# Next block's K projection and first Q projection issued before the channel-mix K product

## The reference

```python
h = _layernorm(x)
q = _rope(h @ Wq.T + bq); k = _rope(h @ Wk.T + bk); v = h @ Wv.T + bv   # 16 heads of 64
a = banded_attention(q, k, v, window=512) @ Wo.T + bo                   # each query sees 512 keys back
x = x + _layernorm(a)
h2 = _layernorm(x)
h2_prev = h2 shifted by one token
xr = mu_r * h2 + (1 - mu_r) * h2_prev
xk = mu_k * h2 + (1 - mu_k) * h2_prev
y = sigmoid(xr @ Wr) * (square(relu(xk @ Wk2)) @ Wv2)
return x + _layernorm(y)
```

## Time and profile before

| | |
|---|---|
| time | 5608.96 us, median of 2 runs (5575.37 and 5642.55) |
| profiled execution | 5639.6 us |
| its span, slowest core (core 4) | 5637.9 us; the cores span 5570.8 to 5637.9 us |
| busy: PE, DVE, ACT, POOL | 59%, 45%, 38%, 19% |
| one block in the middle (core 4) | 347.8 us |
| of it: Q, K and V projection | 59.3 us |
| attention | 122.6 us |
| Wo | 22.0 us |
| from the last Wo to the first Wr matmul | 68.7 us |
| Wr, Wk2, Wv2 | 32.5, 18.7, 24.0 us |

### The profile page before, as it was taken

The page is one execution under the profiler, slowest core; times in us unless marked ns, Lnnn a source line. Parts: engine busy times, 40 slices in busy tenths (PEclk is TensorE's granted clock), DMA queues, the critical chain, the costliest instruction groups (busy, mean ns, idle before and its releaser), DMA issues.

```text
span 5637.9 us, 53990 instructions; the slowest of 8 cores (5570.8 to 5637.9 us)
## 1 busy us (share of the span) xinstructions
PE 3308.2 (59%) x11681; PEld 1268.3 (22%) x11840; DVE 2528.0 (45%) x3689; ACT 2121.4 (38%) x3905; POOL 1066.1 (19%) x900
## 2 busy tenths in 40 slices
PE   0345737467363756738475583865838377383773
PEld 0112313122121322313121231322313122131321
DVE  2354535444363544535445353443535535354352
ACT  0142534426333342533425253352533326243262
POOL 0011212212111121212212121121211212122131
PEclk9957567585676757566575656756567575666756
DMA  6513031130312213031130312203022130311301
GB/s 198 153 37 103 11 88 62 45 105 1 94 56 83 67 45 105 1 90 60 45 105 26 89 36 67 83 30 99 22 71 79 47 103 8 90 53 50 100 8 60
DMA packets 251425, 376.92 MB, mean 67 GB/s; under 512 B 149730, under 2 KB 149730, under 8 KB 251108
## 3 DMA queue, kind: packets, MB, share of 16 engines
q1 hardware_dynamic: 185060, 163.72, 11.3%
q0 software_dynamic: 33792, 134.22, 7.5%
q10 hardware_dynamic: 32256, 75.51, 3.5%
HBM read 264.33 MB, written 75.50 MB: 60 GB/s over the span
## 4 chain that ended last, share of the span: by engine, by line
PE 35%; DVE 20%; ACT 19%; issue 9%; DMA 7%; POOL 5%; SPq 3%; ACTq 2%; DVEq 1%; POOLq 0%
PE pb L477 8%; ACT pk L449 7%; PE pb L442 5%; PE pb L391 5%; DVE ybuf L489 4%; PE pb L653 4%; PE pb L628 4%; ACT vext L249 4%; ACT vext L252 4%; PE pb L533 3%; DVE ax L589 3%; SPq L173 3%; POOL pk L460 2%; POOL ybuf L702 2%; DVE qx L585 2%
## 5 line engine op out<-in xcount | busy, mean ns | idle before, releaser
L489 DVE RECIPROCAL ybuf<-pb 1x512 bf16<-1x512 f32 x256 | 858.0, 3351 | 772.1 <-PE pb L477 763.4
L628 PE MATMUL pb<-WS,qx 128*128 128x512 bf16 x1008 | 305.4, 468 | 1316.9 <-DVE qx L596 1098.0
L449 ACT ACTIVATE pk<-pb,neg 128x512 bf16<-128x512 f32 (+3 forms) x1792 | 945.4, 528 | 282.5 <-PE pb L442 27.9
L442 PE MATMUL pb<-qx,krot 64*128 64x512 bf16 (+3 forms) x1792 | 675.8, 433 | 308.9 <-ACT pk L449 253.7
L477 PE MATMUL pb<-pk,vext 128*65 128x128 bf16 (+3 forms) x2368 | 522.1, 404 | 78.9 <-DVE ax L502 38.8
L628 PEld LDWEIGHTS pb<-WS,qx 128*128 128x128 bf16 x1024 | 112.9, 114 | 1505.4 <-issue 1463.9
L464 POOL TENSOR_TENSOR pk<-pk,tri4s 128x512 bf16<-128x512 bf16 x256 | 294.8, 1151 | 755.3 <-ACT pk L449 755.3
L460 POOL TENSOR_TENSOR pk<-pk,tri0s 128x512 bf16<-128x512 bf16 x192 | 221.1, 1152 | 1126.7 <-ACT pk L449 1126.7
L340 PE MATMUL pb<-hfm,Wwq 128*128 128x512 bf16 x1008 | 271.3, 428 | 266.2 <-DMA hfm<-hstage 223.4
L477 PEld LDWEIGHTS pb<-pk,vext 128*65 128x65 bf16 x2368 | 309.2, 171 | 254.8 <-issue 171.4
L678 PE MATMUL pb<-WS,pk 128*128 128x512 bf16 x992 | 291.5, 460 | 127.7 <-DVE pk L689 64.3
(11 more groups left out here) (97 smaller groups left out, 3896.4 us busy)
## 6 DMA issues: line engine op xcount, KB each, us to landing
xsl<-x SPq DMA_DIRECT2D x128, 512.0 KB, 3.8
WS<-wo_bf POOLq DMA_DIRECT2D x16, 2048.0 KB, 11.4
WS<-wr_bf POOLq DMA_DIRECT2D x16, 2048.0 KB, 18.9
...
```

The lines of the kernel that those rows point to most:

```text
L442: qlo=qlo, qhi=qhi: e.matmul(pb[bk][:, qlo:qhi], ksrc[po:po + 64, BS * md + 128 * tc:BS * md + 128 * (tc + 1)], qx[po:po + 64, BS * md + q ...
L449: texp = cop("scalar", lambda e, bk=bk, c=c, qlo=qlo, qhi=qhi, pku=pku: e.activation(out=pku[:, BS * c + qlo:BS * c + qhi], in_=pb[bk][:, ...
L489: t_rc = cop("vector", lambda e, rb=recipb[uslot], ub=ub: e.reciprocal(rb, pb[ub][64:65, :]), waits=[t_av, buf.get(("recip", uslot)), prev ...
L628: ins = e.matmul(pb[bk][:, :], qx[:, BS * ci + 128 * tj:BS * ci + 128 * (tj + 1)], WS[1][:, D * ci + BS * hh:D * ci + BS * (hh + 1)], star ...
```

## The change

1. `planA(it + 1)` reads the transposed layer norm into `vext[par2]` (the V buffer of the next block) and no longer into `hfm`.
2. A new `planB1(it + 1)` stands between Wr and Wk2: all four K pairs of the next block (banks (4, 5) and (6, 7) in turn) with their four ropes on DVE, and the matmuls of the first Q pair (banks 0 and 1) without their rope.
3. A new `planB2` opens the next block: the rope of the first Q pair, then the Q pairs 1 to 3 in the banks (6, 7), (4, 5), (6, 7), each with its rope, then V. Since its input lies where V is to be written, V now keeps all eight groups in the eight banks; a memset on DVE (the ones column) waits for all of them, and the eight copies on ACT follow it.
4. The tables of cosine and sine are loaded twice in a block, for K and for Q, with one rope and not two between a load and the rope after next.
5. The square after the relu of Wk2 goes from DVE to POOL. Wk2 uses the banks 2 and 3 (before 4 and 5), Wv2 the banks 2 and 3 (before 6 and 7).
6. The unread output of the layer norms goes to `krot[1 - par]`, in the final layer norm to `ax`; waits follow. The waits of the transposing read of `h2` are now the earlier store and the last use of `hfm`. A debug output (`dbg`) is off.

The rotation (`_rope`) and the projection matmuls (`_proj_mms`) have the same instructions as before, apart from the buffer they read.

```diff
+        buf["lnstat"] = t2
...
-    def planA(it2):
+    t_av_last = None
+    t_attn_evac = []
+
+    def planA(it2, av_tok):
         rows0a = (it2 // NB) * S + (it2 % NB) * BS
+        par2 = (it2 % NB) % 2
...
-        t_hr = [dmat("sync", "hfm", hfm[:, BS * c:BS * (c + 1)], hstage[:, 128 * c:128 * (c + 1)],
-                     waits=[t_hw[-1], buf.get("hfm")]) for c in range(8)]
-        return t_ln, t_hw, [t_hr[-1]] * 8
+        hv = vext[par2]
+        t_hr = [dmat("sync", "hfm", hv[:, BS * c:BS * (c + 1)], hstage[:, 128 * c:128 * (c + 1)],
+                     waits=[t_hw[-1], av_tok]) for c in range(8)]
+        return dict(t_ln=t_ln, t_hw=t_hw, t_hr=[t_hr[-1]] * 8, par2=par2, hv=hv)
...
+    def planB1(it2, A, sinkA_tok):
+        n2 = it2 % NB
+        par2 = A["par2"]
+        hv = A["hv"]
+        t_hr = A["t_hr"]
+        t_cos, load_cos = _mk_cos(n2)
+        load_cos(0)
+        load_cos(1)
+        k_toks = []
+        allmm = []
+        for p in range(4):
+            mm = _proj_mms(W["wk"], t_wres["wk"], p, (4, 5) if p % 2 == 0 else (6, 7),
+                           hv, t_hr, extra=[sinkA_tok] if p == 0 else ())
+            allmm += mm
+            k_toks += _rope(t_cos, krot[par2], sinkA_tok, bks, p,
+                            (4, 5) if p % 2 == 0 else (6, 7), mm)
+            if p + 2 <= 3:
+                load_cos(p + 2)
+        q0_mms = _proj_mms(W["wq"], t_wres["wq"], 0, (0, 1), hv, t_hr)
+        allmm += q0_mms
+        kv_tok[par2]["k"] = list(k_toks)
+        return dict(k_toks=k_toks, q0_mms=q0_mms, allmm=allmm, n2=n2, A=A, par2=par2)
+
+    def planB2(B1, qx_free):
+        A = B1["A"]
+        par2 = B1["par2"]
+        hv, t_hr = A["hv"], A["t_hr"]
+        t_cos, load_cos = _mk_cos(B1["n2"])
+        allmm = list(B1["allmm"])
+        q_toks = []
+        load_cos(0)
+        load_cos(1)
+        q_toks += _rope(t_cos, qx, qx_free, bqs, 0, (0, 1), B1["q0_mms"])
+        for p in range(1, 4):
+            if p + 1 <= 3:
+                load_cos(p + 1)
+            mm = _proj_mms(W["wq"], t_wres["wq"], p, (4, 5) if p % 2 == 0 else (6, 7),
+                           hv, t_hr)
+            allmm += mm
+            q_toks += _rope(t_cos, qx, qx_free, bqs, p,
+                            (4, 5) if p % 2 == 0 else (6, 7), mm)
+        v_mms = []
+        for tj in range(4):
+            for hh in range(2):
+                bk = tj * 2 + hh
+                def vmm(e, bk=bk, tj=tj, hh=hh, hv=hv):
+                    for ci in range(8):
+                        e.matmul(pb[bk][:, :],
+                                 hv[:, BS * ci + 128 * tj:BS * ci + 128 * (tj + 1)],
+                                 W["wv"][:, D * ci + BS * hh:D * ci + BS * (hh + 1)],
+                                 start=(ci == 0), stop=False)
+                    return e.matmul(pb[bk][:, :], onesb[:, :], bvr[:, BS * hh:BS * (hh + 1)],
+                                    start=False, stop=True)
+                tm = cop("tensor", vmm, waits=[bank_free[bk], t_wres["wv"], t_bvc, t_ones],
+                         tok=True)
+                v_mms.append((tm, bk, tj, hh))
+                allmm.append(tm)
+        onesap = bass.AP(vext[par2][:, :].tensor, 64, [[4160, 128], [65, 64]])
+        t_or = cop("vector", lambda e, a=onesap: e.memset(a, 1.0),
+                   waits=[t for t in allmm], tok=True)
+        v_toks = []
+        for tm, bk, tj, hh in v_mms:
+            oap = bass.AP(vext[par2][:, :].tensor, 1040 * tj + 520 * hh,
+                          [[4160, 128], [65, 8], [1, 64]])
+            tev = cop("scalar", lambda e, oap=oap, bk=bk: e.copy(oap, pb[bk][:, :]),
+                      waits=[tm, t_or] + [t for t in allmm], tok=True)
+            bank_free[bk] = tev
+            v_toks.append(tev)
+        kv_tok[par2]["v"] = v_toks
+        return q_toks, v_toks
...
-        lnsink[0] = vext[1 - par][:, 0:2048].bitcast(F32)
-        onesap = bass.AP(vext[par][:, :].tensor, 64, [[4160, 128], [65, 64]])
-        ones_restore = cop("vector", lambda e, a=onesap: e.memset(a, 1.0),
-                           waits=[kv_cons[par]], tok=True)
+        lnsink[0] = krot[1 - par][:, 0:2048].bitcast(F32)
...
-        for p in range(4):
-            q_toks += proj_pair(W["wq"], t_wres["wq"], qx, buf.get("qx"), bqs, p,
-                                (0, 1) if p % 2 == 0 else (2, 3))
-            k_toks += proj_pair(W["wk"], t_wres["wk"], krot[par], kv_cons[par], bks, p,
-                                (4, 5) if p % 2 == 0 else (6, 7))
-            if p + 2 <= 3:
-                load_cos(p + 2, n)
...
-                bk = (tj * 2 + hh) % 2
...
-                tev = cop("scalar", lambda e, oap=oap, bk=bk: e.copy(oap, pb[bk][:, :]),
-                          waits=[tmm, ones_restore], tok=True)
...
+        q_toks, v_toks = planB2(B1, prev_tfe)
...
-                      waits=[t_h2w[-1]] + q_toks + k_toks + v_toks + t_sc_all) for c in range(8)]
+                      waits=[t_h2w[-1], buf.get("hfm")]) for c in range(8)]
...
-            pendingA = planA(it + 1)
+            pendingA = planA(it + 1, t_av_last)
...
+        if it + 1 < niter:
+            pendingB = planB1(it + 1, pendingA, buf.get("lnstat"))
+
         t_wv2 = stream_weight("wv2", 1, wr_users)
...
-            bk = 4 + dk % 2
+            bk = 2 + dk % 2
...
-            tka = cop("vector", lambda e, dk=dk: e.tensor_mul(
+            tka = cop("gpsimd", lambda e, dk=dk: e.tensor_mul(
                 pk2[0][:, BS * dk:BS * (dk + 1)], relu_t[:, :], relu_t[:, :]),
                 waits=[trel, buf.get(("pk", 0))] + t_mixk + t_mixr, tok=True)
...
-                bk = 6 + hh
+                bk = 2 + hh
...
+            lnsink[0] = ax[:, 0:2048].bitcast(F32)
...
+        prev_tfe = t_fe_all[-1]
         buf["qx"] = t_fe_all[-1]
-        buf["ax"] = wk2_users[-1]
+        buf["ax"] = buf.get("lnstat")
         buf[("pk", 0)] = wv2_users[-1]
-        buf[("usb", 0)] = t_ka[-1]
-        buf[("usb", 1)] = t_ka[-1]
+        buf[("pk", 1)] = t_mixk[-1]
```

More of the change, by code:

```diff
@@ new lines, in planA, with _mk_cos, load_cos @@
+        return dict(t_ln=t_ln, t_hw=t_hw, t_hr=[t_hr[-1]] * 8, par2=par2, hv=hv)
+    def _mk_cos(n2):
+        t_cos = {}
+        def load_cos(p):
+            slp = p % 2
+            tc1 = dma("sync", "cos%d" % slp, cosb[slp][:, :], cos_d[p, :, n2 * BS:(n2 + 1) * BS],
+                      waits=[buf.get(("cos", slp))])
+            tc2 = dma("sync", "sin%d" % slp, sinb[slp][:, :], sin_d[p, :, n2 * BS:(n2 + 1) * BS],
+                      waits=[buf.get(("cos", slp))])
+            t_cos[p] = (tc1, tc2)
+        return t_cos, load_cos
@@ new lines, in _proj_mms, with mmgroup @@
+    def _proj_mms(wsb, wwait, p, banks, hv, t_hr, extra=()):
+        mm_toks = []
+        for bi, dc in enumerate((p, p + 4)):
+            bk = banks[bi]
+            def mmgroup(e, bk=bk, dc=dc, wsb=wsb, hv=hv):
+                for ci in range(8):
+                    ins = e.matmul(pb[bk][:, :],
+                                   wsb[:, D * ci + 128 * dc:D * ci + 128 * (dc + 1)],
+                                   hv[:, BS * ci:BS * (ci + 1)],
+                                   start=(ci == 0), stop=(ci == 7))
+                return ins
+            mm_toks.append(cop("tensor", mmgroup,
+                               waits=[bank_free[bk], wwait] + t_hr + list(extra), tok=True))
+        return mm_toks
@@ new lines, in _rope @@
+    def _rope(t_cos, dst, dst_free, bias_sb, p, banks, mm_toks):
+        slp = p % 2
+        blo, bhi = banks
+        cw = [t_cos[p][0], t_cos[p][1], t_bq, t_bk, buf.get("scr"), dst_free] + mm_toks
+        cop("vector", lambda e: e.scalar_tensor_tensor(
+            scr[:, 0:BS], pb[blo][:, :], bias_sb[:, p:p + 1], cosb[slp][:, :],
+            ALU.add, ALU.mult), waits=cw)
+        cop("vector", lambda e: e.scalar_tensor_tensor(
+            scr[:, BS:2 * BS], pb[bhi][:, :], bias_sb[:, p + 4:p + 5], sinb[slp][:, :],
+            ALU.add, ALU.mult))
+        t3 = cop("vector", lambda e: e.tensor_sub(
+            dst[:, BS * p:BS * (p + 1)], scr[:, 0:BS], scr[:, BS:2 * BS]), tok=True)
+        cop("vector", lambda e: e.scalar_tensor_tensor(
+            scr[:, 0:BS], pb[blo][:, :], bias_sb[:, p:p + 1], sinb[slp][:, :],
+            ALU.add, ALU.mult))
+        t5 = cop("vector", lambda e: e.scalar_tensor_tensor(
+            scr[:, BS:2 * BS], pb[bhi][:, :], bias_sb[:, p + 4:p + 5], cosb[slp][:, :],
+            ALU.add, ALU.mult), tok=True)
+        t6 = cop("vector", lambda e: e.tensor_add(
+            dst[:, BS * (p + 4):BS * (p + 5)], scr[:, 0:BS], scr[:, BS:2 * BS]), tok=True)
+        bank_free[blo] = t5
+        bank_free[bhi] = t5
+        buf["scr"] = t6
+        buf[("cos", slp)] = t6
+        return [t3, t6]
@@ L307, in build_core @@
+    pendingA = pendingB = None
+    prev_tfe = None
     for it in range(niter):
@@ L318, in build_core @@
             t_wr = stream_weight("wr", 1, [])
-            t_ln, t_hw, t_hr = planA(0)
```

(7 more changed lines are left out.)

46 lines of the change are left out of this document (9 added, 37 removed).

## The result

| | before | changed |
|---|---|---|
| median | 5584.08 us (10 runs) | 5798.38 us (12 runs) |
| lowest and highest | 5575.37 and 5642.55 | 5755.89 and 5879.63 |
| ratio | | 1.0344, 95% interval 1.030 to 1.0388 |
| spans of the cores in the profiled execution | 5570.8 to 5637.9 | 5738.1 to 5754.3 |

By the medians the change costs 214 us; the forecast was 249 us (5858), the range 5770 to 5955. In the profiled execution of the changed kernel the clocks of the eight cores lie between 0.693 and 0.695.

What follows compares the result with a forecast made beforehand. Bound taken: the chain through final layer norm, ropes and V. 15 transitions at 15.6 us (234), first block +14 or 15, last +1, make +249 us on 5608.96: 5858 us, range 5770 to 5955.

Steps and rivals of the forecast that it cites:

- transitions: Passages from one block to the next, 15 in all; each taken as 15.6 us slower, between core 4's +17.5 and core 0's +13.8.
- What bounds the kernel: Between Wk2 and attention, the chain ending last runs through final layer norm, ropes on DVE, then V on PE.
- step 1: Between Wr and Wk2: moved K and Q0 matmuls find no PE gap, are paid in full; +22.3 us on core 4.
- Step 2: In Wk2: square on POOL at 1.15 us, relu-square cycle 2.04 us; +0.7 us on core 4, +3 on core 0.
- The port rule: DVE and GpSimd share ports: first one or two squares beside the last K rope wait some tenths of a us.
- Step 3: Wv2 and final layer norm, first Wv2 matmul to first rope: same instructions in the same order, cost 0.
- Steps 4 and 5: First rope to last projection: only two ropes before Q3, -16.1 us; then Q3 itself at a lower clock, +5.3 (core 4).
- not slower: Rival: Q3's wait far shorter than 14.2 us because the final layer norm finishes sooner; 5657 us, chance 0.08.
- Step 6: Between V and the first exp: all eight V copies follow the last V matmul; +5.3 us, first exp 7.4 after V.
- the stretch: From the first Wk2 matmul to the first exp, 104.2 us on core 4, 99.9 on core 0; all else taken as unchanged.
- looser clock: Rival: longer PE waits loosen the current limit on the clock in dense stages, up to 58.0 us lower; 5800, chance 0.08.

Runs made afterwards that it cites:

- the two experiments on waits: Kernel before, h2 transposing reads waiting only for each list's last token: ratio 0.9841; changed kernel with the old full list of waits back: 1.0526.

## Why the prediction was right, step by step

The time lies in the range and the side is right, and most steps were measured as they were drawn. That the number fits so well is in part luck: had the 100 us of the list of waits stood in the sum, it would have come to 5757, below the range. The omission was offset in part by transitions that cost 18.1 us and not 15.6.

- **What bounds the kernel, and step 1: right.** The chain runs through the final layer norm and the ropes. The K stage takes 20.5 us on a core of full clock (20.2 in the forecast); its bank waits of 0.91 and 2.04 us are where they were drawn. That PE had no gap between Wr and Wk2 was the decisive reading for this stretch. For the whole it is not: with the rest of the change in place, leaving K where it was is slower still (1.0517).
- **Step 2: place right, size too high.** POOL's square takes 1.04 us, not 1.15, the cycle 1.87 and not 2.04; on this core the cost is 1.7 us for a block against the 3 forecast. The port rule that the prediction cites from the Trainium skill ("SBUF — State Buffer", section "SBUF: two separate sides") changes next to nothing here: beside the last K rope the first square took 1.03 us, the others 1.04, and it began 0.27 us after the end of its relu, the others 0.14.
- **Step 3: nearly right**, 1.3 us instead of 0: 38.0 from the first Wv2 matmul to the first rope, 36.8 on core 0; the first tiles ran more slowly behind the longer wait for the square (8.34 against 7.07 us for 32 matmuls).
- **Steps 4 and 5: the trade is right.** Q3 starts 9.55 us after the first rope (9.4), PE waits 16.4 us (14.2), Q3 and V end 31.6 us after the first rope (31.0). But what the wait is worth was read wrongly. The rival "not slower" priced it at 14.2 + 1.1 us for a block, as if V would move forward with Q3. Taking it away gained nothing, because the tables of ropes 2 and 3 were next in line. In step 1 I had costed the later table loads at nothing for K, rightly, and for Q I never asked, though the rows of the landing (5.4 to 8.6 us) against 5.3 us of lead said so, and other cores and blocks of before, up to 15.0 us, still more.
- **Step 6: right.** 7.7 us to the first exp where 7.4 was forecast, and the version with overlapped copies gained what the step says.
- **The step that failed** is the sentence that everything outside the stretch stays as it is. The list of waits in front of the transposing reads was in the diff and was taken as a matter of which event comes last. It was worth 7 us in each of 12 blocks and 4 in 4 others, all on the chain that ends last, 100 us in the change's favour.
- **The balance over all blocks.** Core 6 is 174.4 us longer than core 0 of before. The 15 intervals from Wr to Wr grew by 6.3 to 19.5 us, 167.0 in all: +309 from Wr to Wk2, +28 in Wk2, -152 from the first Wv2 matmul to V's last, +84 from there to exp, +2 in attention and Wo, -104 from Wo to Wr. The start grew by 4.5 us (some 9, and 4.6 given back by the waits; the forecast had 14 or 15) and the end by 2.9 (forecast 1). So without the waits a transition costs 18.1 us, and not the 15.1 of the block shown or the 15.6 of the forecast. The term that was mis-sized is the gain from Wv2 to the end of V, -10.1 us on average where steps 3 to 5 had -14.7 for such a core and the block shown has -12.8. It is smallest in the first and the last interval (-6.0 and -2.7), where the tables landed 13.5 to 16.1 us after their issue and V itself waited for the last rope's banks (2.31 and 3.38 us).
- **What stays open** is why the medians differ by 214 us where these two cores differ by 174 and the lowest times by 181: the runs of the changed kernel spread wider (5756 to 5880), and why was not looked into.
- **The clock.** The rival "looser clock" is not borne out: core 6 has a mean granted clock of 0.693 where core 0 of before has 0.701, so it is not looser, and the two experiments on waits account for the shortfall without it.
